# Attention times V in two row strips of 64 tokens, 64 columns each, the strips writing to different banks

## The chip, the core and the metric

The kernel runs on one core of a Trainium2 chip. The metric is the device time of one execution in microseconds (us), and the median of several executions is quoted. The core's engines run side by side: PE (TensorE) multiplies, and its weight loads are shown apart as PEld; DVE (VectorE), ACT (ScalarE) and POOL (GpSimd) do elementwise work; SP issues most of the DMAs. They meet only at semaphores. PE writes to PSUM, which has eight banks of 512 fp32 columns in each of its 128 partitions.

## The reference

Thirty-two batches of 32 tokens with 512 features go through a mix, an attention block, a state space convolution and a feed-forward block. The change is in the attention, which attends only within a batch of 32 tokens:

```python
q = rms_norm(hidden @ Wq + bq, gq); k = rms_norm(hidden @ Wk + bk, gk); v = hidden @ Wv + bv
# 32 heads of 128 features; B = 32 batches, S = 32 tokens each
attn = softmax(einsum('bhqd,bhkd->bhqk', q, k) / sqrt(128))
out = einsum('bhqk,bhkd->bhqd', attn, v)
x = x + out.reshape(B, S, 4096) @ Wo + bo
```

## The kernel before, in words

The 1024 tokens are eight groups of 128 (`G` = 8, index `g`), a group being four batches. The 32 heads are eight quads of four (`NQ` = 8, `QUAD` = 4, index `t` for the quad, `h` for the head in it).

A first phase makes the scores of all heads. From then on PE runs, quad by quad, `attend(t)`, then `value_group(t + 1, g)` for the eight groups (the next quad's V, 96 matmuls), then `project(t)` (this quad's attention times Wo, 96 matmuls into banks 6 and 7). Every engine has its own program, written out by hand in this order; quads 1 to 3 and 5 to 6 are loops. The last quad has no values to make behind it: `attend(7)` is followed at once by the projection of quad 7, whose weights lie in `wv_hi` and `wv_lo`.

`attend` multiplies V with the softmax weights. For one head and one group the stationary operand is `v_sb[:, g, ...]`, 128 tokens by 128 features, and the moving one is `p_blocks[:, h, g, :]`, 128 tokens by 128 columns (the queries). Since a batch sees only itself, `p_blocks` holds four 32x32 blocks on its diagonal, and the rest of the 128 columns is zero. Both are fp32, and each such matmul stands in the trace as two pairs of a weight load and a matmul, so that one `attend` is 32 matmuls in the program and 64 in the trace. It goes in eight units of four groups, each into one bank (banks 2 to 5 in turn); unit `u` waits until the bank's last content has been read (`alo_ok`).

A unit leaves its bank in two steps: ACT writes `attn_hi` (adding the bias of V), and then DVE reads the bank again and writes the remainder `attn_lo`; the DVE step counts `alo_ok` up. Behind its eight units ACT rounds the quad's Wo into `wo_hi`, and DVE makes `wo_lo` from it (`split_o`). In the last quad `split_o` stands in the middle of the units on both engines, after the fourth, and fills `wv_hi` and `wv_lo`:

```python
attn_out(NQ - 1, range(4))
split_o(NQ - 1, hi=wv_hi, lo=wv_lo, raw=wv_raw)
attn_out(NQ - 1, range(4, 8))
```

On DVE `soft_norm` turns the normalised softmax weights into `p_blocks` with four transposes, one for each batch of a group.

Of the kernel before, what the change touches and what calls it, by code (L numbers as in the profile page):

```python
# [22 lines left out]
F32 = mybir.dt.float32  # L23
F32R = mybir.dt.float32r
I32 = mybir.dt.int32
ALU = mybir.AluOpType
ACT = mybir.ActivationFunctionType
AX_X = mybir.AxisListType.X

P = 128  # L30
BATCH, SEQ, FEAT = 32, 32, 512
TOK = BATCH * SEQ
HEADS, HD = 32, 128
INNER = HEADS * HD
KC = FEAT // P
G = TOK // P
BPG = P // SEQ
HALF = TOK // 2
QUAD = 4
NQ = HEADS // QUAD  # L40
# [21 lines left out]
def build_program(nc, x, cond_idx, lengths, cond_w, wq, bq, wk, bk, wv, bv, wo, bo, gq, gk,  # L62
# [3 lines left out]
    with ctx:  # L66
        def sb(name, shape, dt=F32, scope=ctx):
            return scope.enter_context(nc.sbuf_tensor(name, shape, dt))

        def sem(name):  # L70
            return ctx.enter_context(nc.semaphore(name))

        def overlay(*lots):


            made = []
            for n, lot in enumerate(lots):
                scope = ctx if n == len(lots) - 1 else ExitStack()
                made.append([sb(name, shape, dt, scope) for name, shape, dt in lot])
                if scope is not ctx:  # L80
                    scope.close()
            return made
# [3 lines left out]
        def bank(n, width=512):  # L86
            return psum[:, n * 512:n * 512 + width]
# [22 lines left out]
        def gap(kib):  # L110

            return (f"gap{next(gaps)}", [P, int(kib * KIB)], F32)
# [38 lines left out]
         (ffn_raw,),  # L151
         (t_hi, t_lo, w_raw0, w_hi0, w_lo0, w_raw1, w_hi1, w_lo1, qk_sb, sq, sumsq, bo_rows),
         (ffn_lo, ffn_hi, a_all, b_all, ax, fb_rows, mask, _, x2p, y_t, y_hi, y_lo),
         (wo_lo, wo_hi, _, wv_lo, wv_hi, v_sb, p_blocks, attn_hi, attn_lo)) = overlay(
            [gap(76), ("x_nat", [P, G, FEAT], F32)],
            [("wo_raw", [P, QUAD, FEAT], F32), gap(24), ("wv_raw", [P, KC, 512], F32)],
            [gap(16), ("ang", [P, 67, 32], F32), ("expo", [P, 48, 32], F32), ("mult", [P, 67], F32),
# [12 lines left out]
             ("y_hi", [P, KC, BATCH, SEQ], F32R), ("y_lo", [P, KC, BATCH, SEQ], F32R)],  # L170
            [("wo_lo", [P, QUAD, FEAT], F32R), ("wo_hi", [P, QUAD, FEAT], F32R), gap(16),
             ("wv_lo", [P, KC, 512], F32R), ("wv_hi", [P, KC, 512], F32R), ("v_sb", [P, G, 512], F32),
             ("p_blocks", [P, QUAD, G, P], F32), ("attn_hi", [P, QUAD, TOK], F32R), ("attn_lo", [P, QUAD, TOK], F32R)])
        w_raw, w_hi, w_lo = (w_raw0, w_raw1), (w_hi0, w_hi1), (w_lo0, w_lo1)

        small = sb("small", [P, 16, 32])
# [35 lines left out]
        v_mm, v_ok, pv_mm, ahi_ok, alo_ok = (sem(n) for n in ("v_mm", "v_ok", "pv_mm", "ahi_ok", "alo_ok"))  # L212
# [25 lines left out]
        def repeat(ap, axis, n):  # L238

            dims = [list(d) for d in ap.ap]  # L240
            dims.insert(axis, [0, n])
            return bass.AP(ap.tensor, ap.offset, dims)
# [7 lines left out]

        def quadrant(b):
            return slice(32 * b, 32 * b + 32)

        block = ctx.enter_context(nc.Block())

# [326 lines left out]
        def _(pe):  # L582
            mm = nc.tensor.matmul
# [14 lines left out]
            for n in range(2):  # L598
                last = mm(bank(n), onehot[:].rearrange("n q b -> n (q b)"), cond_nat[:, 512 * n:512 * n + 512],
                          start=True, stop=True)  # L600
# [4 lines left out]
            for g in range(G):  # L605
# [5 lines left out]
                for c in range(KC):  # L611
                    last = mm(bank(2 + g % 6)[:, P * c:P * c + P], x_nat[:, g, P * c:P * c + P],  # L612
                              mix_w[:, g, :], start=True, stop=True)
# [7 lines left out]
            for n in range(9):  # L621
                last = nc.tensor.transpose(bank(1)[:, 32 * n:32 * n + 32], prm_nat[:, n, :], ident[0:32, 0:32])
# [97 lines left out]
            def attend(t, first=False):  # L720

                pe.wait_ge(p_ok, t + 1)
                pe.wait_ge(v_ok, t * G + G)
                for u in range(8):
                    h, half = u % QUAD, u // QUAD
                    if not (first and u < 4):
                        pe.wait_ge(alo_ok, t * 8 + (u - 3))
                    for g in range(4 * half, 4 * half + 4):
                        last = mm(bank(2 + u % 4)[:, P * (g % 4):P * (g % 4) + P],  # L729
                                  v_sb[:, g, HD * h:HD * h + HD], p_blocks[:, h, g, :], start=True, stop=True)  # L730
                    last.then_inc(pv_mm, 1)

            def project_group(t, g, free=True, hi=wo_hi, lo=wo_lo):

                if free:
                    pe.wait_ge(acc_ok, t * 8 + (g - 1))
                tok = slice(P * g, P * g + P)
                product3(bank(6 + g % 2),
                         [(attn_hi[:, h, tok], attn_lo[:, h, tok], hi[:, h, :], lo[:, h, :])
                          for h in range(QUAD)]).then_inc(wo_mm, 1)  # L740
# [16 lines left out]
            for n in range(2):  # L757
                last = mm(bank(2 + n), ones[:, :], sumsq[:, 1, HALF * n:HALF * n + HALF], start=True, stop=True)
            last.then_inc(vk_mm, 1)
            pe.wait_ge(q_sum, HEADS - 1)  # L760
            for g in range(G):
                last = mm(bank(5)[:, g:g + 1], sumsq[:, 0, P * g:P * g + P], ones[:, 0:1], start=True, stop=True)
# [23 lines left out]
            for h in range(SEQ):  # L786
                last = mm(bank(0, 1024)[0:CA, CL * h:CL * h + CL], u_tab[:, :, h], expo[:, 0:CL, h],
                          start=True, stop=True)
# [11 lines left out]
            def transpose_x2(g):  # L800
                pe.wait_ge(acc_ok, 8 * (NQ - 1) + g + 1)
                if g >= 4:
                    pe.wait_ge(x2p_ok, g - 3)
                for c in range(KC):
                    last = nc.tensor.transpose(bank(2 + g % 4)[:, P * c:P * c + P], acc[:, g, P * c:P * c + P],
                                               ident[:, :])
                last.then_inc(xt_mm, 1)

            pe.wait_ge(wolo_ok, NQ)
            for g in range(G):  # L810
                if g % 4 == 0:
                    pe.wait_ge(alo_ok, 8 * (NQ - 1) + 4 + g)
                project_group(NQ - 1, g, hi=wv_hi, lo=wv_lo)
                if g >= 2:
                    transpose_x2(g - 2)
# [74 lines left out]
        def _(act):  # L890
            sc = nc.scalar
# [4 lines left out]
            def here(index):  # L896
                if isinstance(index, int):
                    return index
                act.reg_mov(spacer, index)
                return act.snap(spacer, min_val=0, max_val=HEADS - 1)  # L900
# [136 lines left out]
            def attn_out(t, units=range(8)):  # L1037

                for u in units:
                    h, half = u % QUAD, u // QUAD  # L1040
                    act.wait_ge(pv_mm, t * 8 + (u + 1))
                    at = here(t * QUAD + h)
                    sc.activation(attn_hi[:, h, HALF * half:HALF * half + HALF], bank(2 + u % 4), ACT.Identity,  # L1043
                                  bias=params[:, PARAM["bv"], bass.ds(at, 1)]).then_inc(ahi_ok, 1)

            def split_o(t, hi=wo_hi, raw=wo_raw):
# [77 lines left out]
        def _(dve):  # L1124
            v = nc.vector
# [34 lines left out]
            for b in range(BPG):  # L1160
                last = v.tensor_copy(mix_w[quadrant(b), :, quadrant(b)],
                                     mix_t[quadrant(b)].rearrange("p d (g b) -> p g d b", b=BPG)[:, :, :, b])
# [151 lines left out]
            def flat(tile):  # L1314
                return tile[:].rearrange("p h g k -> p (h g) k")
# [12 lines left out]
            def soft_norm(t):  # L1328

                dve.wait_ge(e_ok, t + 1)  # L1330
                v.tensor_reduce(row_sum[:], flat(sm_s), AX_X, ALU.add).then_inc(soft, 1)
                dve.wait_ge(soft, t * 6 + 4)
                v.reciprocal(row_inv[:], row_sum[:]).then_inc(soft, 1)
                dve.wait_ge(soft, t * 6 + 5)
                v.tensor_tensor(flat(sm_s), flat(sm_s), repeat(row_inv[:], 2, 32), ALU.mult).then_inc(soft, 1)
                dve.wait_ge(soft, t * 6 + 6)
                dve.wait_ge(pv_mm, t * 8) if not isinstance(t, int) or t > 0 else None
                for b in range(BPG):
                    last = v.transpose(p_blocks[quadrant(b), :, :, quadrant(b)].rearrange("p h g q -> p (h g) q"),  # L1339
                                       sm_s[quadrant(b)].rearrange("p h g k -> p (h g) k"))  # L1340
                last.then_inc(p_ok, 1)

# [5 lines left out]
            def attn_out(t, units=range(8)):  # L1348

                for u in units:  # L1350
                    h, half = u % QUAD, u // QUAD
                    tok = slice(HALF * half, HALF * half + HALF)
                    dve.wait_ge(ahi_ok, t * 8 + (u + 1))
                    v.scalar_tensor_tensor(attn_lo[:, h, tok], bank(2 + u % 4),
                                           params[:, PARAM["bv"], bass.ds(t * QUAD + h, 1)],
                                           attn_hi[:, h, tok].bitcast(F32), ALU.add, ALU.subtract).then_inc(alo_ok, 1)

            def split_o(t, hi=wo_hi, lo=wo_lo, raw=wo_raw):
                dve.wait_ge(wohi_ok, t + 1)
# [59 lines left out]
            for g in range(G):  # L1419
                half = slice(2 * RANK * (g % 2), 2 * RANK * (g % 2) + 2 * RANK)  # L1420
# [43 lines left out]
```

## Time and profile before

| | before |
|---|---|
| median of 3 executions | 914.47 us (911.4 to 914.81) |
| the profiled execution | 912.63 us, of which the span shown in the profile is 910.8 us |
| PE busy | 865.6 us, 95% of the span |
| DVE, POOL, ACT busy | 592.7, 418.8, 378.3 us |
| mean granted TensorE clock | 0.985 of full speed |

The span runs from the first to the last recorded instruction; the profiled execution's own time is 1.8 us longer. Matmuls are pipelined, and the ends of their records are modelled, so the duration of one record is longer than the distance to the next one; what a stream of them costs is read from the distances, which the chain of waits shows as time per group of instructions.

### The profile page before, as it was taken

The numbers are of one execution on the slowest core, as the hardware profiler recorded it, in microseconds if no ns is written. First come the engines' busy times: TensorE is split into PE (matmuls) and PEld (weight loads), VectorE is DVE, ScalarE is ACT, GpSimd is POOL, SyncE is SP. The second block draws the span as 40 slices with busy tenths as digits, with TensorE's granted clock in tenths as the row PEclk, the third lists the DMA queues.
The fourth block names the chain that finished last, engine by engine and source line by source line (L and its number), as shares of the span: only waits on it lengthen the run. The fifth ranks groups of instructions, "written<-read, shape, count | busy, mean of one in ns | idle before, by whom it ended". The sixth has DMA issues, their size and how long they took to land.

```text
span 910.8 us, 12373 instructions
## 1 busy us (share of the span) xinstructions
PE 865.6 (95%) x4529; PEld 721.2 (79%) x4529; DVE 592.7 (65%) x650; ACT 378.3 (42%) x492; POOL 418.8 (46%) x401
## 2 busy tenths in 40 slices
PE   6598799999999999999799899999999999999998
PEld 4487688888888888887788788888888888888465
DVE  4976677777777777776765366576477766453421
ACT  3453466666556555654522514232141413132400
POOL 0778922222222222209998072999279960000500
PEclk9899899999999999999899999999999999999999
DMA  5016011111111111101111015111221111438301
GB/s 168 24 49 164 23 47 47 47 47 49 48 47 48 49 48 48 45 32 44 47 46 47 1 47 93 46 46 46 69 24 47 47 47 49 151 127 247 89 22 71
DMA packets 83569, 56.50 MB, mean 62 GB/s; under 512 B 33638, under 2 KB 66758, under 8 KB 83414
## 3 DMA queue, kind: packets, MB, share of 16 engines
q1 hardware_dynamic: 82576, 55.67, 21.1%
q10 hardware_dynamic: 966, 0.48, 0.2%
q8 instruction: 17, 0.28, 0.1%
q14 instruction: 10, 0.08, 0.0%
HBM read 52.32 MB, written 3.82 MB: 62 GB/s over the span
## 4 chain that ended last, share of the span: by engine, by line
PE 85%; POOL 4%; DVE 4%; ACT 3%; DMA 1%; issue 1%; ACTq 0%; SPq 0%; POOLq 0%; DVEq 0%
PE psum L590 13%; PE psum L591 13%; PE psum L592 13%; PE psum L636 10%; PE psum L637 10%; PE psum L638 10%; PE psum L729 6%; PE psum L669 5%; PE psum L833 2%; PE psum L862 1%; DVE w_lo L1151 1%; PE psum L884 1%; PE psum L612 1%; POOL small L450 1%; DMA wv_raw<-in_wv 1%
## 5 line engine op out<-in xcount | busy, mean ns | idle before, releaser
L430 POOL TENSOR_TENSOR w_raw<-w_raw 128x256 f32<-128x256 f32 x30 | 24.3, 808 | 195.8 <-DMA w_raw<-in_wk 195.6
L636 PE MATMUL psum<-t_hi,w_hi 128*128 128x512 f32 x256 | 103.5, 404 | 7.3 <-DVE t_lo L1197 7.3
L1369 DVE TENSOR_TENSOR acc<-psum,acc 128x512 f32<-128x512 f32 x64 | 44.2, 690 | 92.6 <-PE psum L592 92.4
L590 PE MATMUL psum<-wv_hi,mix_hi 128*128 128x512 f32 x256 | 101.1, 395 | 2.9 <-ACT v_sb L1031 2.9
L637 PE MATMUL psum<-t_lo,w_hi 128*128 128x512 f32 x256 | 100.5, 393 | 0.0
L638 PE MATMUL psum<-t_hi,w_lo 128*128 128x512 f32 x256 | 100.4, 392 | 0.0
L591 PE MATMUL psum<-wv_lo,mix_hi 128*128 128x512 f32 x256 | 100.4, 392 | 0.0
L592 PE MATMUL psum<-wv_hi,mix_lo 128*128 128x512 f32 x256 | 100.3, 392 | 0.0
L1043 ACT ACTIVATE attn_hi<-psum,params 128x512 fp32r<-128x512 f32 x64 | 43.7, 688 | 110.3 <-PE psum L729 109.8
L636 PE MATMUL psum<-mix_hi,w_hi 128*128 128x512 f32 x192 | 76.2, 397 | 11.8 <-DVE w_lo L1151 10.1
L591 PE MATMUL psum<-wo_lo,attn_hi 128*128 128x512 f32 x224 | 87.1, 389 | 0.0
L590 PE MATMUL psum<-wo_hi,attn_hi 128*128 128x512 f32 x224 | 87.1, 389 | 0.0
L592 PE MATMUL psum<-wo_hi,attn_lo 128*128 128x512 f32 x224 | 87.1, 389 | 0.0
L1031 ACT ACTIVATE v_sb<-psum 128x512 f32<-128x512 f32 x64 | 38.2, 598 | 106.5 <-PE psum L592 106.0
L1239 DVE TENSOR_TENSOR sumsq<-sumsq,sq 128x1024 f32<-128x1024 f32 x62 | 76.3, 1231 | 0.0
L638 PE MATMUL psum<-mix_hi,w_lo 128*128 128x512 f32 x192 | 75.7, 394 | 0.0
L637 PE MATMUL psum<-mix_lo,w_hi 128*128 128x512 f32 x192 | 75.7, 394 | 0.0
L1011 ACT ACTIVATE sq<-qk_sb 128x1024 f32<-128x1024 f32 x31 | 32.7, 1056 | 99.7 <-issue 96.1
L1151 DVE TENSOR_TENSOR w_lo<-w_raw,w_hi 128x1792 fp32r<-128x1792 f32 x32 | 67.1, 2097 | 8.9 <-ACT w_hi L917 8.9
L729 PE MATMUL psum<-p_blocks,v_sb 128*128 128x128 f32 x512 | 61.5, 283 | 4.7 <-DVE p_blocks L1339 4.5
L729 PEld LDWEIGHTS psum<-p_blocks,v_sb 128*128 128x128 f32 x512 | 60.9, 199 | 5.8 <-issue 4.9
L669 PEld LDWEIGHTS psum<-qk_sb 128*128 128x128 f32 x512 | 62.0, 191 | 3.8 <-issue 1.4
(233 smaller groups left out, 1913.7 us busy)
## 6 DMA issues: line engine op xcount, KB each, us to landing
w_raw<-in_wq SPq DMA_DIRECT2D x32, 256.0 KB, 2.9
w_raw<-in_wk SPq DMA_DIRECT2D x32, 256.0 KB, 3.2
wv_raw<-in_wv SPq DMA_DIRECT2D x8, 1024.0 KB, 5.5
toep<-kpad_dram SPq DMA_DIRECT2D x2, 4096.0 KB, 15.4
wo_raw<-in_wo SPq DMA_DIRECT2D x7, 1024.0 KB, 5.4
x_nat<-in_x SPq DMA_DIRECT2D x4, 512.0 KB, 6.2
acc<-in_x SPq DMA_DIRECT2D x1, 2048.0 KB, 10.7
out_dram<-o_stage SPq DMA_DIRECT2D x8, 256.0 KB, 2.0
```

Source lines behind the costliest of these rows:

```text
L590: mm(out, lh, rh, start=(n == 0), stop=False)
L591: mm(out, lh, rl, start=False, stop=False)
L592: last = mm(out, ll, rh, start=False, stop=(close and n == len(terms) - 1))
L636: mm(bank(n), wh, hi[:, c, tok], start=(i == 0), stop=False)
L637: mm(bank(n), wh, lo[:, c, tok], start=False, stop=False)
L638: last = mm(bank(n), wl, hi[:, c, tok], start=False, stop=(i == 1))
L669: last = mm(bank(6, 1024)[:, P * g:P * g + P], qk_sb[:, slot, 0, P * g:P * g + P], qk_sb[:, slot, 1, P * g:P * g + P], start=True, stop=True)
L729: last = mm(bank(2 + u % 4)[:, P * (g % 4):P * (g % 4) + P], v_sb[:, g, HD * h:HD * h + HD], p_blocks[:, h, g, :], start=True, stop=True)
L1043: sc.activation(attn_hi[:, h, HALF * half:HALF * half + HALF], bank(2 + u % 4), ACT.Identity, bias=params[:, PARAM["bv"], bass.ds(at, 1)]) ...
L1151: v.tensor_tensor(w_lo[slot][:].rearrange("p b n -> p (b n)"), w_raw[slot][:, 1:8, :].rearrange("p b n -> p (b n)"), w_hi[slot][:].rearran ...
L1239: v.tensor_tensor(sumsq[:, m, :], sumsq[:, m, :], sq[:, m, :], ALU.add).then_inc(total, 1)
L1369: v.tensor_tensor(acc[:, g, :], bank(6 + g % 2), acc[:, g, :], ALU.add).then_inc(acc_ok, 1)
```

## The change

`attend` uses the array in two row strips of 64: rows 0 to 63 (`tile_position` (0, 0)) hold tokens 0 to 63 of a group, that is two batches, and rows 64 to 127 (`tile_position` (64, 0)) the other two. Each strip multiplies its 64 tokens of V by a 64 x 64 block of `p_blocks`, so a matmul has 64 moving columns. `p_blocks` is half as large, and a gap keeps the other tiles where they were. There are 64 such matmuls in an `attend`, 128 in the trace, and they alternate between the strips. A bank now holds one head and one strip: 8 groups x 64 columns. Head `h` fills banks 2 and 3 or 4 and 5, and waits for `alo_ok` once for both. The unit `u` on ACT and DVE is head `u // 2`, strip `u % 2`, and its output goes to eight pieces of 64 columns. The last projection waits for all of `attn_lo` before its first matmul, where it waited for half of it before.

```diff
@@ overlay
-             ("p_blocks", [P, QUAD, G, P], F32), ("attn_hi", [P, QUAD, TOK], F32R), ("attn_lo", [P, QUAD, TOK], F32R)])
+             ("p_blocks", [P, QUAD, G, 2 * SEQ], F32), gap(8), ("attn_hi", [P, QUAD, TOK], F32R), ("attn_lo", [P, QUAD, TOK], F32R)])
+        def pair_rows(tile, h, r):
+            return tile[:, h, :].rearrange("p (g r q) -> p g r q", g=G, r=2)[:, :, r, :]
@@ attend (PE)
-                for u in range(8):
-                    h, half = u % QUAD, u // QUAD
-                    if not (first and u < 4):
-                        pe.wait_ge(alo_ok, t * 8 + (u - 3))
-                    for g in range(4 * half, 4 * half + 4):
-                        last = mm(bank(2 + u % 4)[:, P * (g % 4):P * (g % 4) + P],
-                                  v_sb[:, g, HD * h:HD * h + HD], p_blocks[:, h, g, :], start=True, stop=True)
-                    last.then_inc(pv_mm, 1)
+                for h in range(QUAD):
+                    if not (first and h < 2):
+                        pe.wait_ge(alo_ok, t * 8 + (2 * h - 2))
+                    for g in range(G):
+                        for r in range(2):
+                            rows = slice(64 * r, 64 * r + 64)
+                            last = mm(bank(2 + 2 * (h % 2) + r)[:, 64 * g:64 * g + 64], v_sb[rows, g, HD * h:HD * h + HD],
+                                      p_blocks[rows, h, g, :], start=True, stop=True, tile_position=(64 * r, 0))
+                            if g == G - 1:
+                                last.then_inc(pv_mm, 1)
@@ the last projection (PE)
             pe.wait_ge(wolo_ok, NQ)
+            pe.wait_ge(alo_ok, 8 * NQ)
             for g in range(G):
-                if g % 4 == 0:
-                    pe.wait_ge(alo_ok, 8 * (NQ - 1) + 4 + g)
@@ attn_out (ACT; DVE alike with attn_lo)
-                    sc.activation(attn_hi[:, h, HALF * half:HALF * half + HALF], bank(2 + u % 4), ACT.Identity,
+                    sc.activation(pair_rows(attn_hi, h, r), bank(2 + u % 4).rearrange("p (g q) -> p g q", g=G), ACT.Identity,
@@ soft_norm (DVE)
-                    last = v.transpose(p_blocks[quadrant(b), :, :, quadrant(b)].rearrange("p h g q -> p (h g) q"),
+                    last = v.transpose(p_blocks[quadrant(b), :, :, quadrant(b % 2)].rearrange("p h g q -> p (h g) q"),
```

The first place is PE's program of the last quad, from `attend(7)` to the projection. Names are the tiles read; a number behind an x counts equal rows (each a matmul of the program). Before, first the start of the attention, where two units stand, and then its last unit with the projection's first and fifth group:

```order
L729 MATMUL psum<-p_blocks,v_sb 128x128 [waits alo_ok,v_ok,p_ok]
L729 MATMUL psum<-p_blocks,v_sb 128x128 x3
L729 MATMUL psum<-p_blocks,v_sb 128x128 [waits alo_ok]
L729 MATMUL psum<-p_blocks,v_sb 128x128 x3
...
L590 MATMUL psum<-wv_hi,attn_hi 128x512 [waits acc_ok,alo_ok,wolo_ok]
L591 MATMUL psum<-wv_lo,attn_hi 128x512
...
L590 MATMUL psum<-wv_hi,attn_hi 128x512 [waits acc_ok,alo_ok]
```

And now, the whole of `attend(7)` and the projection's first group:

```order
L734 MATMUL psum<-p_blocks,v_sb 128x64 [waits alo_ok,v_ok,p_ok]
L734 MATMUL psum<-p_blocks,v_sb 128x64 x15
L734 MATMUL psum<-p_blocks,v_sb 128x64 [waits alo_ok]
L734 MATMUL psum<-p_blocks,v_sb 128x64 x15
...
L594 MATMUL psum<-wv_hi,attn_hi 128x512 [waits acc_ok,alo_ok,wolo_ok]
L595 MATMUL psum<-wv_lo,attn_hi 128x512
```

Eight waits on `alo_ok`, one in four matmuls, have become four, one in sixteen; of the projection's two waits on `alo_ok` the one on its fifth group is gone, and the first now asks for all eight units.

The second place is DVE's program around the last quad's units, before:

```order
L1369 TENSOR_TENSOR acc<-psum,acc 128x512 [waits acc_ok,wo_mm] x8
L1354 SCALAR_TENSOR_TENSOR attn_lo<-psum,params,attn_hi 128x512 [waits ahi_ok] x4
L1360 TENSOR_TENSOR wv_lo<-wv_raw,wv_hi 128x2048 [waits wohi_ok]
L1354 SCALAR_TENSOR_TENSOR attn_lo<-psum,params,attn_hi 128x512 [waits ahi_ok] x4
L1392 STREAM_TRANSPOSE a_turn<-a_sum 128x1024 [waits lora]
```

And now:

```order
L1373 TENSOR_TENSOR acc<-psum,acc 128x512 [waits acc_ok,wo_mm] x8
L1358 SCALAR_TENSOR_TENSOR attn_lo<-psum,params,attn_hi 128x8x64 [waits ahi_ok] x4
L1364 TENSOR_TENSOR wv_lo<-wv_raw,wv_hi 128x2048 [waits wohi_ok]
L1358 SCALAR_TENSOR_TENSOR attn_lo<-psum,params,attn_hi 128x8x64 [waits ahi_ok] x4
L1396 STREAM_TRANSPOSE a_turn<-a_sum 128x1024 [waits lora]
```

Nothing has moved on DVE (nor on ACT, POOL and SP): the units have another shape, and `wv_lo` still stands between the fourth and the fifth of them.

## Rows read from the trace of the kernel before

**Rows 1.** The page: busy time by engine, and shares of the chain that ended last

```profile
PE 865.6 (95%) x4529; PEld 721.2 (79%) x4529; DVE 592.7 (65%) x650; ACT 378.3 (42%) x492; POOL 418.8 (46%) x401
PE 85%; POOL 4%; DVE 4%; ACT 3%; DMA 1%; issue 1%; ACTq 0%; SPq 0%; POOLq 0%; DVEq 0%
```

**Rows 2.** Chain in order of time, second half (start us, us, what)

```profile
447.62 3.84 PE psum L729 x32
495.03 7.14 PE psum L729 x64
...
808.06 3.58 PE psum L729 x32
...
812.36 1.81 ACT wv_hi L1048
814.19 2.30 DVE wv_lo L1360
```

**Rows 3.** Same chain: fp32 matmuls of 1 column, 512, 32 (16-column weights)

```profile
416.72 1.72 PE psum L758 x4
418.44 1.68 PE psum L762 x16
651.88 3.92 PE psum L787 x64
```

**Rows 4.** Weight loads of four lines (duration ns min/median/max, first and last start)

```profile
L599 PEld LDWEIGHTS psum<-cond_nat,onehot x4: 282/330/332, 5.8 to 7.7; 16*128 16x128 f32 x4
L612 PEld LDWEIGHTS psum<-mix_w,x_nat x64: 192/192/338, 12.5 to 21.4; 128*128 128x128 f32 x64
L833 PEld LDWEIGHTS psum<-toep,x2p x256: 106/110/110, 844.3 to 865.9; 128*32 128x32 f32 x128
```

**Rows 5.** Chain again: convolution in four column strips, transposes between, and transposes elsewhere

```profile
825.05 0.44 PE psum L805 x4
...
851.90 0.59 PE psum L845 x4
852.49 2.29 PE psum L833 x32
```

**Rows 6.** Timeline of the first weight loads of such a convolution (start us, us, instruction)

```profile
849.54 0.16 PEld L833 LDWEIGHTS psum<-toep,x2p 128*32 128x32 f32 x8 [0.17 <-issue]
```

**Rows 7.** Timeline of attend(1): PE, ACT's first two units, DVE

```profile
494.87 7.30 PE L729 MATMUL psum<-p_blocks,v_sb 128*128 128x128 f32 x64
495.95 0.69 ACT L1043 ACTIVATE attn_hi<-psum,params 128x512 fp32r<-128x512 f32 x1 [15.04 <-PE psum L729]
496.85 0.69 ACT L1043 ACTIVATE attn_hi<-psum,params 128x512 fp32r<-128x512 f32 x1 [0.21 <-PE psum L729]
496.81 2.51 DVE L1354 SCALAR_TENSOR_TENSOR attn_lo<-psum,params,attn_hi 128x512 fp32r<-128x512 f32 x3 [1.06 <-ACT attn_hi L1043]
```

**Rows 8.** Timeline after attend(7): ACT, DVE, PE

```profile
814.05 2.41 ACT L1043 ACTIVATE attn_hi<-psum,params 128x512 fp32r<-128x512 f32 x4
816.39 2.72 DVE L1354 SCALAR_TENSOR_TENSOR attn_lo<-psum,params,attn_hi 128x512 fp32r<-128x512 f32 x4
816.53 0.50 PE L590 MATMUL psum<-wv_hi,attn_hi 128*128 128x512 f32 x1 [1.33 <-DVE wv_lo L1360]
```

**Rows 9.** Timeline: PE after its two longer idle times, DVE in attend(0)

```profile
441.08 10.38 PE L729 MATMUL psum<-p_blocks,v_sb 128*128 128x128 f32 x64 [4.51 <-DVE p_blocks L1339]
446.83 6.14 DVE L1354 SCALAR_TENSOR_TENSOR attn_lo<-psum,params,attn_hi 128x512 fp32r<-128x512 f32 x8
524.13 0.50 PE L590 MATMUL psum<-wv_hi,mix_hi 128*128 128x512 f32 x1 [2.90 <-ACT v_sb L1031]
```

**Rows 10.** Windows (from:to, length, busy by engine, PEclk the granted clock, DMA)

```profile
441.00:446.60 5.60, 5.52 (x26) 5.55 (x27) 2.60 (x4) 3.20 (x4) 5.35 (x4) 0.51 0.03 11
525.00:528.50 3.50, 3.50 (x10) 2.72 (x9) 3.32 (x4) 0.00 (x0) 2.86 (x9) 0.51 0.02 5
816.50:824.80 8.30, 8.27 (x36) 6.74 (x37) 6.16 (x8) 0.00 (x0) 0.00 (x0) 1.00 0.25 39
```

More of the change, by code:

```diff
@@ L153, in build_program @@
          (ffn_lo, ffn_hi, a_all, b_all, ax, fb_rows, mask, _, x2p, y_t, y_hi, y_lo),
-         (wo_lo, wo_hi, _, wv_lo, wv_hi, v_sb, p_blocks, attn_hi, attn_lo)) = overlay(
+         (wo_lo, wo_hi, _, wv_lo, wv_hi, v_sb, p_blocks, _, attn_hi, attn_lo)) = overlay(
             [gap(76), ("x_nat", [P, G, FEAT], F32)],
@@ L1039, in attn_out @@
                 for u in units:
-                    h, half = u % QUAD, u // QUAD
+                    h, r = u // 2, u % 2
                     act.wait_ge(pv_mm, t * 8 + (u + 1))
                     at = here(t * QUAD + h)
-                    sc.activation(attn_hi[:, h, HALF * half:HALF * half + HALF], bank(2 + u % 4), ACT.Identity,
+                    sc.activation(pair_rows(attn_hi, h, r), bank(2 + u % 4).rearrange("p (g q) -> p g q", g=G), ACT.Identity,
                                   bias=params[:, PARAM["bv"], bass.ds(at, 1)]).then_inc(ahi_ok, 1)
@@ L1350, in attn_out @@
                 for u in units:
-                    h, half = u % QUAD, u // QUAD
-                    tok = slice(HALF * half, HALF * half + HALF)
+                    h, r = u // 2, u % 2
                     dve.wait_ge(ahi_ok, t * 8 + (u + 1))
-                    v.scalar_tensor_tensor(attn_lo[:, h, tok], bank(2 + u % 4),
+                    v.scalar_tensor_tensor(pair_rows(attn_lo, h, r), bank(2 + u % 4).rearrange("p (g q) -> p g q", g=G),
                                            params[:, PARAM["bv"], bass.ds(t * QUAD + h, 1)],
-                                           attn_hi[:, h, tok].bitcast(F32), ALU.add, ALU.subtract).then_inc(alo_ok, 1)
+                                           pair_rows(attn_hi, h, r).bitcast(F32), ALU.add, ALU.subtract).then_inc(alo_ok, 1)
             def split_o(t, hi=wo_hi, lo=wo_lo, raw=wo_raw):
```

## The prediction

> **What bounds the kernel now.** I read the page first: PE is busy 95% of the span, and the chain of work that ended last is PE for 85% of it [rows 1]. So the kernel's time is PE's time plus the few stretches where PE waits, and the reader should look at what PE's stretches of attention times V (line 729) cost and what ends the waits beside them. The chain in order of time gives that: after the first, which has its own start, six of them stand as one piece of 7.14 us each (495.03 is the first of the six), with no gap before or behind; of the last one 3.58 us are on the chain, and then ACT's and DVE's rounding of Wo, until PE goes on at 816.53 [rows 2, 8]. All eight together are some 57 us, 6% of the span: that is all that the change can work on.
>
> Then I asked what limits one such piece. 7.14 us over 64 pairs of weight load and matmul is 111.6 ns a pair. The moving side alone would be 128 columns; the four matmuls of 512 columns cost 1.72 us, 430 ns each or 0.84 ns a column [rows 3], so 128 columns are 107 ns. But line 762 moves a single column against weights of 128 columns, and its 16 pairs cost 1.68 us, 105 ns each [rows 3]. With 16 weight columns and 32 moving ones a pair costs 3.92/64 = 61 ns [rows 3]. So a pair with 128 weight columns costs 105 ns or more however few columns move: the weight load is as tight a limit as the matmul. The change halves the matmul and not the load.
>
> **What the change does to PE's stream.** Removed: 64 pairs per attention, each with 128 rows, 128 weight columns, 128 moving columns. Added: 128 pairs with 64 rows, 128 weight columns, 64 moving columns, half in each strip. No row shows a row strip. The bounds of a strip's price:
>
> - Does a load of 64 rows cost less? At the slower clock of the kernel's start the loads of line 599, of 16 rows, take 330 ns, and the longest of line 612, of 128 rows, take 338; loads with 32 weight columns take 110 where 128 take 192 at full clock [rows 4]. So columns set a load's time, rows don't. I charge a strip's load like a whole one, 111.6 ns, the price of a pair in the attention now. The rule of the Trainium skill that speaks against this change is the one on LDWEIGHTS in "TensorE: Matmul & The Clock Gate": P/1.2 ns, P being the columns and the contraction dimension of no account. By it alone a strip's pair would be an estimated 107 ns and the sum 64 x 8 x 4.9 ns = 2.5 us lower; the row decides.
> - Do the two strips load at the same time? Upper bound: one after the other, 128 x 111.6 = 14.28 us per attention. Lower bound: together, 64 x 111.6 = 7.14 us, as before. The nearest rows are the convolution's, in four column strips: eight loads start and end within 0.16 us, one of them taking 110 ns, and 32 pairs cost 2.29 us [rows 4 to 6]. One strip's eight matmuls there have 2 x (512 + 384 + 256 + 128) = 2560 columns, 2.15 us; four strips in a row would be 8.6 us. So strips overlap almost fully, loads among them. I take 7.14 us. What is against it: those are column strips, with 32 weight columns each, and eight such loads in a row would also fit beside the matmuls. The Trainium skill, "TensorEngine Tiling (Array Packing)", Key Properties, states that different tiles can load and multiply in parallel; no row here shows that for row strips, and by it the sum is the one below.
> - The change of the array's partition. Four transposes between two convolutions cost 0.59 us, and 0.44 elsewhere [rows 5]: 0.15 for one way. The convolution is 2.29 - 2.15 = 0.14 over its columns. I put 0.29 us on each attention; nothing hides it, PE being the chain. Bounds 0 and 0.6.
>
> **The banks.** Before, a bank was full every 0.89 us and wanted again 2.7 us later. Now two banks fill together, at 16 x 111.6 = 1.79 us after the start, and head 2 wants them both at 3.57. What happens between, from [rows 7, 8]: ACT starts 495.95 - 494.87 - 0.89 = 0.19 us behind the last matmul, takes 0.69, DVE starts 0.17 later and takes 0.68 for each of two units (2.72/4), and PE goes 0.04 behind DVE (814.19 + 2.30 to 816.53, [rows 2, 8]): 1.79 + 0.19 + 0.69 + 0.17 + 1.36 + 0.04 = 4.24. PE waits 0.67 us, and then one load of 0.11 lies open. Head 3 asks at 4.24 + 0.11 + 1.79 = 6.14 for banks that DVE leaves at 3.57 + 0.19 + 0.69 + 0.17 + 1.36 + 0.04 = 6.02: no wait, with 0.12 to spare. Queued behind the waiting matmul is all of PE's program, so it goes to the end in full. Each of attentions 1 to 6: 0.67 + 0.11 + 0.29 = 1.07 us, six of them **+6.4**.
>
> **Attention 0** starts at 441.08 at half clock, and DVE, which has `wv_lo` to make, begins its units only at 446.83 [rows 9, 10]. Head 2 then starts at 446.83 + 1.36 + 0.04 = 448.2 and the end is 448.2 + 0.11 + 3.57 + 0.15 = 452.1, against 447.62 + 3.84 = 451.46 [rows 2]: **+0.6**.
>
> **The last projection.** Before it starts behind `wv_lo`, with four units of `attn_lo` done and four still running on DVE to 819.1 beside it [rows 8]. Now it waits for all eight. From 808.06: heads 0 and 1 end at 808.06 + 0.14 + 3.57 = 811.8; ACT's units 2 and 3 end at 812.0 + 0.69 + 0.60 = 813.3, its `wv_hi` (some 1.9) at 815.2, DVE's `wv_lo` (2.30) at 817.5, its last four units (2.72) at 820.2, and PE starts at 820.2 where it started at 816.53: **+3.7**. ACT's last four units end at 815.2 + 2.41 = 817.6, in time.
>
> **The clock.** PE then idles from about 816.1 to 820.2, 4.1 us, where it idled 1.33. Idle times of 4.51 and 2.90 us were followed by stretches at a granted clock of 0.51, that is at 1.2 instead of 2.4 GHz, of 5.6 and 3.5 us; 1.33 was not [rows 8 to 10]. Half of such a stretch is lost: 1.7 to 2.8 us. I take **+2.0**; lower bound 0.
>
> **Costed at nothing.** POOL clears a smaller `p_blocks`, long before it is used. The four transposes on DVE write as many elements as before. ACT's and DVE's units move the same 512 columns, in eight pieces of 64; if that made them slower, DVE's 0.68 goes twice into head 2's wait. Behind each attention DVE and ACT finish some 0.4 us later against PE's end, covered by 96 matmuls of values (over 21 us); only the last quad lacks that cover, and it is counted.
>
> **Sum.** 6.4 + 0.6 + 3.7 + 2.0 = 12.7 us on the profiled execution's 912.63: 925.3 us. That execution lies 1.8 below the median of the three; on the median the sum would be 927.2. I say 925.3.
>
> **Rivals.**
>
> - *The strips load one after the other.* For it: half as much weight per load is no help [rows 4], and no row shows two loads of 128 columns overlapping. Each of six attentions costs 14.28 + 0.29 - 7.14 = 7.43 us more (no wait for banks, a head taking 3.57), together 44.6. The first: 5.5 us at half clock hold 25 pairs, the other 103 cost 11.5, and it ends at 458.3, +6.8. The last ends at 822.5, its last two units leave DVE at 824.9, +8.4, without the clock's fall. Sum 59.8: 972.4 us. Between it and the forecast each 10 ns on a strip's pair are 64 x 8 x 10 ns = 5.1 us. Chance 0.18.
> - *Not slower: the load isn't the limit in a strip.* If a pair of a strip costs 61 ns, as with few weight columns [rows 3], a head takes 0.98 us, and DVE sets the pace: it starts at 0.98 + 0.19 + 0.69 + 0.17 = 2.03, head 2 at 3.43, head 3 at 4.79, and the end is at 0.98 + 0.11 + 0.29 more, 6.17 us instead of 7.14. Six times that is -5.8, the first -0.7, the last projection still +2.3 (DVE's `wv_lo` ends at 816.1 and its four units at 818.9) and the clock +2.0: 910.4 us, no change; 908.4 without the clock's fall. It decides from about 80 ns a pair downward. The 105 ns of a single column speak against it [rows 3]. Chance 0.10. Beside it stands the Trainium skill's page "TensorEngine Tiling (Array Packing)", Theoretical Speedup, which promises up to 2x for a contraction of 64; taken whole that would be this rival, and no row here bears it out for weights of 128 columns.
> - *The strips save the wait.* If a bank wait were shorter than I say (ACT and DVE at their fastest), 6.4 goes to 1.7: 920.6. That lies in the forecast's own range.
>
> **How the numbers follow.** The forecast has 0.72, and its own range is 917 (no cost of the partition and no fall of the clock: 925.3 - 2.4 - 2.0 - 3 for shorter waits) to 934 (0.6 for the partition, the clock's 2.8, head 3 waiting too, the median's 1.8). With the rival that isn't slower, down to 908, and pairs partly overlapped, up to 938, the range holds about 0.8; the serial case is left out. Half a per cent, 4.6 us, is about what can be told from no change. Faster by more than that needs less than 908: 0.04. Within it, 0.10. Slower, 0.86.
>
> **What the profile after would show.** Line 734: 1024 matmuls, and a strip's pair every 112 ns (the two strips together one every 56), an attention of about 8.2 us on the chain; 6.2 us would be the fallen load limit, 14.6 the serial rival. PE waiting for DVE's `attn_lo` about 0.7 us once in each attention, at head 2. PE's first matmul of the last projection 3.7 us later against the attention's start, released by `attn_lo` and not by `wv_lo`, and a granted clock of 0.5 behind it. The prediction is wrong above all if a strip's load has another price than 112 ns or the strips don't load together, since each attention holds 64 of them in each strip.

## The result and the profile after

The changed kernel takes 946.17 us (median of 4, 945.76 to 947.99) against 913.12 us of the kernel before (4 runs): a ratio of 1.0366, 95% interval 1.0338 to 1.0394. The forecast had 925.3 us and a range up to 938: right in its direction, far too small in its size. The profiled execution took 945.76 us, with a span of 944.0.

The page of the kernel after: busy time by engine, the chain's shares by engine, and the attention's two groups (line 734) with their mean durations and the idle time ahead of them:

```profile
PE 890.4 (94%) x5041; PEld 739.8 (78%) x5041; DVE 588.1 (62%) x650; ACT 374.8 (40%) x492; POOL 416.4 (44%) x401
PEclk9899899999999999997798999989899899999999
PE 84%; DVE 5%; POOL 4%; ACT 3%; issue 2%; DMA 1%; ACTq 0%; DVEq 0%; SPq 0%; POOLq 0%
L734 PE MATMUL psum<-p_blocks,v_sb 64*128 64x64 f32 x1024 | 73.9, 310 | 10.4 <-DVE attn_lo L1358 7.1
L734 PEld LDWEIGHTS psum<-p_blocks,v_sb 64*128 64x128 f32 x1024 | 71.4, 223 | 14.1 <-DVE attn_lo L1358 8.2
```

PE is still busy 94% of a longer span, as in [rows 1]. The second line is the one that a reader of busy shares would skip: behind the first five slices the granted clock has six slices below 9, where the kernel before had one, and the engine rows don't show it. Over the whole span the mean clock is 0.958, where it was 0.985. With two levels, 1 and 0.5 (2.4 and 1.2 GHz), that is 2 x 0.042 x 944 = 79 us at half clock, where it was 2 x 0.015 x 911 = 27.

Attention 6 is an undisturbed one. Its timeline on PE and on DVE:

```profile
784.07 3.79 PE L734 MATMUL psum<-p_blocks,v_sb 64*128 64x64 f32 x64
788.28 3.79 PE L734 MATMUL psum<-p_blocks,v_sb 64*128 64x64 f32 x64 [0.43 <-DVE attn_lo L1358]
792.00 0.50 PE L594 MATMUL psum<-wv_hi,mix_hi 128*128 128x512 f32 x1
786.82 1.41 DVE L1358 SCALAR_TENSOR_TENSOR attn_lo<-psum,params,attn_hi 128x512 fp32r<-128x512 f32 x2 [1.95 <-ACT attn_hi L1048]
```

Two heads are 64 pairs in 3.6 us or so, one every 56 ns: the strips do load and multiply at the same time, at 112 ns a pair in each. Head 2 starts 4.21 us after head 0, and DVE's two reads of the first banks end its wait. The whole attention is 7.93 us from its first matmul to the first one behind it. The kernel before had 7.06 between the same two places (its window, from:to, length, PE busy, PEclk, DMA share, GB/s; the 7.14 and 7.30 of [rows 2, 7] are read from other points of the records):

```profile
494.87:501.93 7.06, 7.06 (x66) 1.00 0.52 151
```

Attention 1 starts in the same way and ends otherwise. Its pieces on the chain (start us, us, what), with the next values behind it:

```profile
501.24 1.98 PE psum L734 x32
503.22 0.68 ACT attn_hi L1048
...
504.72 0.75 DVE attn_lo L1358
505.48 0.04 issue
505.52 5.69 PE psum L734 x64
511.21 0.72 PE psum L594
511.93 0.43 PE psum L595
```

The second half takes 5.69 us, and the value matmuls behind it 0.43 instead of 0.23. The windows say why (columns as above; attentions 0, 1, 2, 4 and 6, then the stage behind attention 4, and the start of the last projection):

```profile
439.08:455.76 16.68, 14.11 (x128) 0.50 0.09 33
501.17:511.14 9.97, 9.41 (x129) 0.80 0.32 107
560.83:569.11 8.28, 7.51 (x129) 1.00 0.84 191
672.03:682.57 10.54, 9.77 (x130) 0.77 0.84 133
784.07:792.00 7.93, 7.50 (x129) 1.00 0.45 141
682.57:728.80 46.23, 46.23 (x194) 0.94 0.07 23
847.69:856.00 8.31, 8.31 (x28) 0.75 0.55 84
```

The clock falls to 1.2 GHz in attentions 1, 3, 4 and 5 and takes part of the next stage with it; attentions 2 and 6 keep full clock; attention 0 runs wholly at half clock. Its two halves on PE:

```profile
439.08 7.09 PE L734 MATMUL psum<-p_blocks,v_sb 64*128 64x64 f32 x64 [3.28 <-DVE p_blocks L1344]
448.74 7.09 PE L734 MATMUL psum<-p_blocks,v_sb 64*128 64x64 f32 x64 [2.57 <-DVE attn_lo L1358]
```

The excess of the span, 944.0 - 910.8 = 33.2 us, splits at the stages' first matmuls as follows (attention: from its first matmul to the next stage's first):

| part | forecast | measured |
|---|---|---|
| before attention 0 (starts at 439.08, before at 441.08) | 0 | -2.0 |
| attention 0: 10.14 to 16.68 us | +0.6 | +6.5 |
| attentions 1 to 6: 42.5 to 55.7 us in all | +6.4 | +13.3 |
| attention 7 with the gap behind it: 8.63 to 11.94 | +3.7 | +3.3 |
| values and projections between the attentions: 314.2 to 324.2 | 0 | +10.0 |
| from the last projection on | +2.0 | +2.0 |
| sum | +12.7 | +33.1 |

The first row is in part the change's own. PE's idle time before attention 0 is 3.3 us in all five strip kernels of this document and 4.5 in all five whole-array ones. POOL clears the smaller `p_blocks` in 1.81 us instead of 3.52, ends its two long products 2.5 us earlier (418.69 against 421.17), and DVE's softmax has shorter instructions there (`inv_norm` 0.42 us instead of 0.97); that the one causes the other was not tested. The other 0.8 us of the 2.0 are no effect of the edit: the kernel before has them too when it is run with another edit far behind (the earlier split below).

### The profile page after: what moved, and what is told of

The parts are those of the page before. It is cut to its first block, busy times and chain, and to the rows that moved or that the text cites. A ratio compares the mean times of both kernels' runs of the same rounds, so it can differ in the third digit from the quotient of the medians.

```text
span 944.0 us, 13391 instructions
## 1 busy us (share of the span) xinstructions
PE 890.4 (94%) x5041; PEld 739.8 (78%) x5041; DVE 588.1 (62%) x650; ACT 374.8 (40%) x492; POOL 416.4 (44%) x401
## 4 chain that ended last, share of the span: by engine, by line
PE 84%; DVE 5%; POOL 4%; ACT 3%; issue 2%; DMA 1%; ACTq 0%; DVEq 0%; SPq 0%; POOLq 0%
PE psum L594 14%; PE psum L595 13%; PE psum L596 13%; PE psum L640 9%; PE psum L642 9%; PE psum L641 9%; PE psum L734 6%; PE psum L673 5%; PE psum L838 1%; PE psum L867 1%; DVE w_lo L1156 1%; PE psum L889 1%; DVE attn_lo L1358 1%; DVE wv_lo L1250 1%; DMA wv_raw<-in_wv 1%
## 5 line engine op out<-in xcount | busy, mean ns | idle before, releaser
L594 PE MATMUL psum<-wv_hi,mix_hi 128*128 128x512 f32 x256 | 105.7, 413 | 2.9 <-ACT v_sb L1036 2.9
L595 PE MATMUL psum<-wv_lo,mix_hi 128*128 128x512 f32 x256 | 103.7, 405 | 0.0
L596 PE MATMUL psum<-wv_hi,mix_lo 128*128 128x512 f32 x256 | 103.5, 404 | 0.0
L1048 ACT ACTIVATE attn_hi<-psum,params 128x512 fp32r<-128x512 f32 x64 | 40.5, 684 | 136.5 <-PE psum L734 136.5
L734 PE MATMUL psum<-p_blocks,v_sb 64*128 64x64 f32 x1024 | 73.9, 310 | 10.4 <-DVE attn_lo L1358 7.1
L734 PEld LDWEIGHTS psum<-p_blocks,v_sb 64*128 64x128 f32 x1024 | 71.4, 223 | 14.1 <-DVE attn_lo L1358 8.2
L1358 DVE SCALAR_TENSOR_TENSOR attn_lo<-psum,params,attn_hi 128x512 fp32r<-128x512 f32 x64 | 44.9, 746 | 43.3 <-ACT attn_hi L1048 43.3
## 6 DMA issues: line engine op xcount, KB each, us to landing
acc<-in_x SPq DMA_DIRECT2D x1, 2048.0 KB, 10.4
```

The lines of the kernel that those rows point to most:

```text
L594: mm(out, lh, rh, start=(n == 0), stop=False)
L595: mm(out, lh, rl, start=False, stop=False)
L596: last = mm(out, ll, rh, start=False, stop=(close and n == len(terms) - 1))
L734: last = mm(bank(2 + 2 * (h % 2) + r)[:, 64 * g:64 * g + 64], v_sb[rows, g, HD * h:HD * h + HD], p_blocks[rows, h, g, :], start=True, stop ...
L1358: v.scalar_tensor_tensor(pair_rows(attn_lo, h, r), bank(2 + u % 4).rearrange("p (g q) -> p g q", g=G), params[:, PARAM["bv"], bass.ds(t * ...
```

## Experiments: what brings the clock down

Two things are new in an attention: the matmuls move 64 columns in the time of a load of 128, and PE waits once for the banks. Theory A has the first alone bring the clock down, theory B the second alone. Four kernels ran on one chip with the kernel before at 912.77 us (7 runs). In all of them a pair costs 112 ns at full clock, as forecast.

**No wait.** The changed kernel, heads 2 and 3 in other banks (ACT and DVE read them there, not shown):

```diff
+                base = (2, 4, 6, 2)
...
-                    if not (first and h < 2):
-                        pe.wait_ge(alo_ok, t * 8 + (2 * h - 2))
+                    if h == 2:
+                        pe.wait_ge(s_ok, HEADS) if first else pe.wait_ge(acc_ok, t * 8)
+                    elif h == 3:
+                        pe.wait_ge(alo_ok, t * 8 + 2)
+                    elif not first:
+                        pe.wait_ge(alo_ok, t * 8)
...
-                            last = mm(bank(2 + 2 * (h % 2) + r)[:, 64 * g:64 * g + 64], v_sb[rows, g, HD * h:HD * h + HD],
+                            last = mm(bank(base[h] + r)[:, 64 * g:64 * g + 64], v_sb[rows, g, HD * h:HD * h + HD],
```

> The changed kernel with head 2 of each attention in banks 6 and 7 and head 3 in banks 2 and 3, so that no head waits for a bank that is being read. Theory A (the clock falls because the strips with 64 moving columns leave the array's streaming side half empty): the wait goes, an attention at full clock takes about 7.4 us, but the granted clock still falls to half in or behind most attentions; about 940 us, 5 to 6 below the changed kernel's 946. Theory B (the clock falls because of the 0.7 to 1 us of PE idle time at head 2): the clock stays up in attentions 1 to 6, and the time goes to about 920 us.

Measured: 923.37 us (ratio to the kernel before 1.0118, 1.01 to 1.0136). Its windows: attention 0, attention 5, the stage behind that, the start of the last projection:

```profile
438.95:452.81 13.86, 13.86 (x129) 0.50 0.10 38
710.79:718.08 7.29, 7.29 (x129) 1.00 0.41 146
718.08:761.80 43.72, 43.72 (x194) 1.00 0.07 25
824.82:832.00 7.18, 7.18 (x25) 0.79 0.49 75
```

The clock stays up through attentions 1 to 6, which speaks for B; 23 us are gone, of which the waits themselves are some 6. But attention 0, which begins at half clock, never leaves it, although it has no wait any more: B alone doesn't give that. The windows also price the strips themselves, at full clock and without a wait: 7.29 - 7.06 = 0.23 us in the attention, and from one attention's start to the next 51.04 us instead of 50.68, so 0.36 in all (the kernel before, then this one, attention 5 to 6):

```profile
706.54:757.22 50.68, 50.68 (x258) 1.00 0.12 42
710.79:761.83 51.04, 51.04 (x321) 1.00 0.12 42
```

**128 moving columns.** The changed kernel with its waits. Each strip's matmul moves its block and the next group's (the last group's only its own); the surplus is overwritten by the next matmul:

```diff
-                            last = mm(bank(2 + 2 * (h % 2) + r)[:, 64 * g:64 * g + 64], v_sb[rows, g, HD * h:HD * h + HD],
-                                      p_blocks[rows, h, g, :], start=True, stop=True, tile_position=(64 * r, 0))
+                            n = min(2, G - g)
+                            last = mm(bank(2 + 2 * (h % 2) + r)[:, 64 * g:64 * g + 64 * n], v_sb[rows, g, HD * h:HD * h + HD],
+                                      p_blocks[rows, h, g:g + n, :].rearrange("p g q -> p (g q)"), start=True, stop=True,
+                                      tile_position=(64 * r, 0))
```

> The changed kernel, with its waits, but each strip's matmul moves 128 columns (the group's block and the next group's; the surplus half of the output is overwritten by the next matmul, so the output is complete). A strip's pair has 107 ns of moving columns and should still cost 112 ns. Theory A (half empty streaming): the clock stays up behind attentions 1 to 6; about 925 us, which is what the prediction had for the change. Theory B (idle at head 2): the waits are the same, the clock falls as before, 946 us. If the two strips shared the moving side, an attention would take about 14 us instead.

Measured: 929.53 us (1.0184, 1.0167 to 1.0201). Attention 0, attention 5 and the stage behind it:

```profile
438.90:454.03 15.13, 10.65 (x128) 0.78 0.10 37
715.72:724.00 8.28, 7.51 (x130) 1.00 0.40 129
724.00:767.70 43.70, 43.70 (x194) 1.00 0.08 25
```

Twice the columns make the kernel 17 us faster. An attention costs what it costs undisturbed in the changed kernel, 8.28 us, with its wait; the clock stays up in attentions 1 to 6, which speaks for A. Neither theory alone can be right: each cure works while the other cause stays. Attention 0 comes back to full clock here, and falls a second time behind a wait of 4.48 us. The load limit shows too: double columns, same time.

**64 columns in the whole array.** The kernel before, no strips and no waits. It leaves out half of the product's columns, and ACT and DVE read the other half twice:

```diff
-                        last = mm(bank(2 + u % 4)[:, P * (g % 4):P * (g % 4) + P],
-                                  v_sb[:, g, HD * h:HD * h + HD], p_blocks[:, h, g, :], start=True, stop=True)
+                        last = mm(bank(2 + u % 4)[:, 64 * (g % 4):64 * (g % 4) + 64],
+                                  v_sb[:, g, HD * h:HD * h + HD], p_blocks[:, h, g, 0:64], start=True, stop=True)
```

> The kernel before, whole array, no strips, with 64 moving columns in each matmul of attention times V instead of 128; it leaves out half of that product's columns and writes the other half twice, so its output is not the reference's. Weight loads are unchanged. If the load is the limit, an attention stays at 7.1 us; if it is not, it falls to about 4 us and the kernel to about 890. Theory A: the clock falls in or behind the attentions although there are no strips and no waits; 925 to 940 us. Theory B: the clock stays up, 913 us.

Measured: 919.23 us (1.0065, 1.0047 to 1.0084), between what A and what B gave it. Attention 0, attention 5, and the start of the last projection:

```profile
441.83:455.48 13.65, 13.64 (x65) 0.50 0.02 7
711.80:718.86 7.06, 7.06 (x66) 1.00 0.40 149
821.81:830.10 8.29, 8.29 (x29) 0.79 0.25 39
```

Half of the moving columns save nothing: 7.06 us, to a hundredth what the kernel before had. So the moving side isn't the limit, and with [rows 3] the load is. The clock behaves as without the wait in strips: up in attentions 1 to 6, and in attention 0 down to its end, where the kernel before was back at full clock after 5.6 us [rows 10]. The third window holds the first sign of both causes together: PE idles 1.33 us before the last projection, as in the kernel before. Behind full columns the clock stayed up there (1.00, [rows 8, 10]), behind half of them it fell (0.79).

**A wait with full columns.** The kernel before, its fifth and sixth units waiting for three units to be read instead of one and two:

```diff
-                        pe.wait_ge(alo_ok, t * 8 + (u - 3))
+                        pe.wait_ge(alo_ok, t * 8 + (3 if u == 4 else max(u - 3, 3) if u > 4 else u - 3))
```

> The kernel before with one wait of about 0.9 us in the middle of each attention: its fifth unit waits until three units have been read instead of one. Streaming is full. Theory A: the clock stays up, and the time is 913 plus eight waits, about 920 us. Theory B: the clock falls behind most attentions, 935 to 945 us.

Measured: 919.39 us (1.0069, 1.005 to 1.0088). Attention 0, attention 5 and the stage behind it:

```profile
441.86:453.26 11.40, 10.03 (x64) 0.76 0.02 7
711.93:720.24 8.31, 7.33 (x65) 1.00 0.34 126
720.24:763.80 43.56, 43.56 (x195) 1.00 0.08 25
```

It costs its waits and nothing else; 0.7 to 1.0 us of idle time with full columns around it doesn't touch the clock in any of attentions 1 to 6.

**Both together, without strips.** Theory C, formed from these four: at full clock it takes half-empty matmuls and an idle piece together; once the clock is down, half-empty matmuls alone keep it there. (Half-empty: with half of the moving columns that fit into the time of their weight load.) The next four ran beside the kernel before at 913.22 us (18 runs). This one is the 64-column kernel above with the wait above, and also leaves out half of the product:

```diff
+                        pe.wait_ge(alo_ok, t * 8 + (3 if u == 4 else max(u - 3, 3) if u > 4 else u - 3))
...
+                                  v_sb[:, g, HD * h:HD * h + HD], p_blocks[:, h, g, 0:64], start=True, stop=True)
```

> The kernel before, whole array, no strips, with both ingredients: 64 moving columns as in e3_full64 (half of the product's columns left out, the other half written twice) and the wait of about 1 us in the middle of each attention as in e4_full_stall. Theory C (it takes half empty streaming and an idle piece together to bring the clock down): the clock falls in or behind most of attentions 1 to 6, and the time is far more than the sum of the two excesses (919.2 + 919.4 - 912.8 = 925.8), 935 to 945 us. Rival (the two strips themselves matter, for example through the change of the array's partition): the clock stays up behind attentions 1 to 6, about 926 us.

Measured: 952.62 us (1.0435, 1.0414 to 1.0456), above even the 935 to 945 that C gave it. Attention 0, attention 5 and the stage behind it:

```profile
440.93:455.86 14.93, 13.91 (x65) 0.50 0.02 8
733.84:744.13 10.29, 9.31 (x65) 0.79 0.28 102
744.13:788.90 44.77, 44.77 (x194) 0.97 0.07 24
```

Two edits that cost 6 to 7 us each cost 39 together, more than the change itself, in a kernel without strips. The clock falls in each of attentions 1 to 7. So it doesn't take strips; in the changed kernel they brought both ingredients.

All medians together, the kernel before being 912.77 beside the first four kernels and 913.22 beside the others:

| matmuls of attention | no wait | wait of about 1 us |
|---|---|---|
| whole array, 128 columns | 913.22 (before) | 919.39 |
| whole array, 64 columns (half left out) | 919.23 | 952.62 |
| strips, 64 columns | 923.37 | 946.17 (after) |
| strips, 128 columns | 915.65 (below, with an earlier split of Wo) | 929.53 |

## Experiments: the last projection and what is left for strips

**Earlier split, kernel before.** The last quad's Wo is there long before, and ACT and DVE have time for it during the projection of quad 6 (DVE's old place between the units goes too, not shown):

```diff
@@ ACT
-            attn_out(NQ - 1, range(4))
             split_o(NQ - 1, hi=wv_hi, raw=wv_raw)
-            attn_out(NQ - 1, range(4, 8))
+            attn_out(NQ - 1)
@@ DVE, in quad(NQ - 2, split=False)
                     if split:
                         split_v(t + 2, (c,))
+                    elif c == 0:
+                        split_o(NQ - 1, hi=wv_hi, lo=wv_lo, raw=wv_raw)
```

> The kernel before with the last quad's split of Wo ahead of its units of attention instead of between them. PE's gap of 1.6 us before the last projection goes; about 911.2 us. If something else ends that gap, no change.

Measured: 910.42 us (median of 10; 0.9974, 0.996 to 0.9989), and attention 7 takes 7.06 us to the projection's first matmul, with no gap, where it took 8.63. That is 1.6 of the 2.8 us between the medians; the rest lies within the spread of the single executions (908.46 to 914.0):

```profile
807.33:814.39 7.06, 7.06 (x66) 1.00 0.49 151
```

**The same edit in the changed kernel.**

> The changed kernel with the same edit. The gap before the last projection goes from 4.2 to about 2.4 us, since all eight units must be in attn_lo and the last two start when the attention ends: 1.8 us less, and up to 3.4 more if the clock then stays up there; 941 to 944 us.

Measured: 945.11 us (1.0351, 1.0331 to 1.0371). Attention 7, and the start of the last projection:

```profile
838.97:849.23 10.26, 7.57 (x129) 0.96 0.28 104
849.23:857.00 7.77, 7.77 (x22) 0.62 0.52 80
```

Attention 7 with its gap shrinks by 1.7 of the expected 1.8 us (11.94 to 10.26), but the clock still falls, some 0.8 us before the projection starts (0.96 over attention 7); the projection's first 8 us have 0.62 instead of 0.75. So of the possible further 3.4 us nothing came, some of the 1.7 is lost again, and the median, 1.1 lower, misses the expected 941 to 944. This run is a weak one: by its interval it can't be told from the changed kernel.

**Strips with all three cures:** the other banks, 128 columns, the earlier split.

> The strips with 128 moving columns, with no wait for banks and with the early split. An attention takes 7.3 us, the clock stays up, attention 0 recovers as in the kernel before; left are 0.23 us an attention for the array's partition and a gap of about 2.4 us before the last projection: about 915.5 us. If the strips had a gain of their own, it would be below 911.

Measured: 915.65 us (median of 9; 1.0027, 1.0015 to 1.0039). Attention 5, and the start of the last projection:

```profile
707.13:714.42 7.29, 7.29 (x129) 1.00 0.45 146
818.83:827.10 8.27, 8.27 (x36) 1.00 0.55 84
```

The clock stays up in attentions 1 to 7 and in the last projection, and yet the strips stand 2.4 us above the kernel before and 5.2 above it with the same early split. The losses that the two traces show: 0.36 us for each of attentions 1 to 6 with the stage behind it; 818.83 - 809.21 = 9.6 us for attention 7 with its gap instead of 7.06, since the projection needs all eight units; and 12.8 us (438.88 to 451.69) for attention 0 instead of 10.4 (440.31 to 450.68). Together that is 7.2 us. Against it stand the earlier start of attention 0 (1.4) and the stage behind attention 1, where the clock fell in the kernel before and not here (47.05 us instead of 48.44); what is left, 4.4, is the difference of the two spans, 913.1 - 908.7. No attention is faster for being in strips.

## Why the prediction missed

- *The load is the limit, and rows don't shorten it* [rows 3, 4]: right. The profile has no granted clock for the kernel's start; that it was slower there rests on loads of one line, 338 and 192 ns. The whole array with 64 columns takes the same 7.06 us, the strips with 64 or 128 columns the same 112 ns a pair.
- *The strips load together* [rows 5, 6]: right, now with weights of 128 columns: 128 pairs in 7.29 us. The serial rival (972 us) is out, and so is the rival that isn't slower. The Trainium skill, "TensorEngine Tiling (Array Packing)", Key Properties, states that different tiles can load and multiply in parallel; the trace agrees. Under Theoretical Speedup the same page of the Trainium skill gives up to 2x for a dimension of 64 or less; for these weights of 128 columns no run bears that out (7.29 us against 7.06).
- *The change of partition, 0.29 us*: the strips cost 0.36 at full clock without a wait, 0.23 in the attention and 0.13 in the stage behind. In mid-stream a strip's pair costs the 112 ns of the kernel before, so the price lies at the two ends; that it is the partition and nothing else was not isolated. The 7.14 us "each" of the six attentions are 7.34 in one of them (attention 4, from 655.80).
- *The banks*: head 2 was said to start 4.24 us after the first matmul and did so after 4.21 (attention 6), 4.35 (attention 1) and 4.55 (attentions 2 to 5); an undisturbed attention is 7.9 to 8.3 us against the forecast's 7.06 + 1.07 = 8.13. The third rival, no bank wait, fell as well.
- *The last projection, +3.7*: measured +3.3, and the clock behind it +2.0, as said. *POOL's smaller `p_blocks`*, costed at nothing, goes with 1.2 us less idle time before attention 0.
- *The step that failed* is the clock's term, +2.0 for the last projection alone. The paragraph on the clock asked only where PE idles for long, after the last attention, and took [rows 9, 10] for the whole law; the attentions and the stages between them were costed as if at full clock, though their matmuls had become half-empty and had a wait among them. The runs showed instead 79 - 27 = 52 us more at half clock, worth up to 26 us. Attentions 1 to 6 measured 6.9 us more than the forecast. The stages between, forecast at 0, cost 10.0, of which the strips' ends are 7 x 0.13 = 0.9. Attention 0 was given +0.6 and ended 4.5 later than before (455.76 against 451.22, its start being 2.0 earlier); heads 2 and 3 alone took 7.02 us (448.74 to 455.76), where they take 3.7 in attention 6. These three make 6.9 + 10.0 + 3.9 = 20.8 us; the last projection's gap, 3.3 instead of 3.7, takes 0.4 back, and the miss in the sum was 33.1 - 12.7 = 20.4.
- The forecast's number was met by another kernel: with 128 moving columns and everything else as changed, 929.53 us against 925.3, inside the 917 to 934 that it gave its own case. The forecast priced a kernel whose clock stays up in attentions 1 to 6 and the stages behind them.

What stays open: attentions 2 and 6 of the changed kernel kept full clock with the same wait (8.28 and 7.93 us), and did so again in the run with the earlier split, whereas it fell in all of attentions 1 to 7 in the whole-array kernel with both edits. The length of the wait doesn't sort these cases: PE idled 0.56 us in attention 1 (9.97 - 9.41) and the clock fell, 0.77 in attention 2 (8.28 - 7.51) and it stayed up. No run varied the length of the wait, or its place in time, alone. Both ingredients also lower the number of columns moved in a stretch of time; whether that number alone is the cause, no run here separates.

The same holds for [rows 9, 10], from which the forecast took its rule. The idle time of 2.90 us behind attention 1 stands in all ten kernels of this document. In the profiled executions of eight of them the clock fell at its end, for 3.4 or 6.8 us, and in two, the whole array with the wait and the strips with all three cures, it did not (the stage behind attention 1 in these two):

```profile
505.02:551.96 46.94, 44.04 (x196) 1.00 0.07 23
503.04:550.09 47.05, 44.15 (x194) 1.00 0.07 23
```

So a single fall, or its absence, proves little; the argument above rests on the counts. At full clock with one ingredient alone the clock fell in none of attentions 1 to 6 (four kernels); with both it fell in four of the six in each of two strip kernels, and in all six in the whole array.

## What to carry to other kernels

Before shortening the moving side of a matmul, or cutting the array into row strips for a short contraction, ask what a pair with one moving column costs: if it is the same, the weight load is the limit and nothing is gained. A matmul emptied in this way isn't free either. Count each wait beside it as a possible fall of the clock for this stage and the next, and judge a change by the granted clock of both, since the busy shares stayed at 94 to 95% through a loss of 33 us. Two edits that are nearly harmless alone (+6.5 and +6.6 us) cost 39 together here, so a suspected cause has to be taken out of the slow kernel as well as put into the fast one.

## What the runs showed of the hardware

Surplus columns that are overwritten later can make a kernel faster: in the strips 128 moving columns instead of 64 took 946.2 to 929.5 us. At full clock, 7 us of pairs with half of their columns left the clock alone, 0.4 to 1.0 us of idle time among full ones did too, and both together brought it to half in most attentions (0.77 to 0.86 over attentions 1, 3, 4 and 5 of the changed kernel). Once it was at half, as in attention 0, full matmuls came back to full clock within the attention (after 5.6 us in the kernel before [rows 10]; PEclk 0.76 with a wait of 1.4 us in it), and half-empty ones did not in 13.6 to 16.7 us (0.50), in strips and in the whole array alike.
